# Five loads of the second tile of x as two transfers each, of 120 and of 8 partitions

## The chip, the cores and the metric

The kernel runs on one core of one Trainium2 chip. The metric is the device time of one execution in microseconds (us). The same core has five engines (PE for matrix work, DVE for elementwise work, ACT for copies here, POOL, and SP, which here issues DMAs and nothing else) and 16 DMA engines, which move data between the chip's large memory (HBM) and the on-chip buffer with its 128 partitions.

## The reference

```
# x: (512, 40, 128) float32, W: (128, 128) float32
proj = jnp.einsum('bnd,ed->bne', x, W)
out = proj[:, PAIR_I, :] * proj[:, PAIR_J, :]     # PAIR_I, PAIR_J = np.triu_indices(40, k=1)
```

Each of the 40 features of a batch row is projected by W, and then every one of the 780 pairs of features is multiplied element by element. The output is 512 x 780 x 128 float32, 204.47 MB, against 10.5 MB of input.

## The kernel before

The batch is worked off in four tiles of 128 rows; row b of a tile lives in partition b. A tile of x is 40 features x 128 values per partition. It comes in as ten loads of four features each (`LOADS`, `LOAD_FEATURES`), the last features first: a load moves 2048 bytes (4 x 128 float32) to each of 128 partitions, 256 KB in all. Two buffers, `x_in[0]` and `x_in[1]`, hold an even and an odd tile. Each of the 20 loads (two tiles of ten) has its own semaphore, `x_loaded[half][load]`; a finished transfer adds 16 to it.

- SP issues all 20 loads of the first two tiles first, in one go and without a wait (line 137). After that its loop over the tiles runs: for each of 20 chunks of 39 pairs it waits until DVE has made the chunk (`chunk_ready`) and issues its store (line 145), 19968 bytes from each of 128 partitions, 2496 KB. There are 80 stores. SP's loads and stores stand in one queue.
- ACT issues the loads of the third and fourth tile (line 211), each once the part of the buffer that it overwrites has been read. They stand in ACT's own queue.
- PE turns each feature (line 172, `turn`, which waits for the feature's load at the first of the two groups of a load) and projects it (line 182). ACT copies the results out of the accumulation banks (lines 206 and 217) into `proj`.
- DVE multiplies (line 248). A chunk is written into one of five slots of `products`, and before a slot is written again DVE waits until the store that last read it has landed completely (`stored[slot]`).

SP's last instructions wait until all 80 stores have landed, and that ends the kernel.

Every transfer is cut into packets that the 16 DMA engines work off. A transfer of 128 partitions has 128 data packets, one for each partition, and 16 small packets behind them, one for each DMA engine, that mark the end of that engine's share in the semaphore (called end marks below; a packet of data is 2048 bytes for a load and 19968 bytes for a store).

Of the kernel before, what the change touches and what calls it, by code (L numbers as in the profile page):

```python
# [5 lines left out]
P = 128  # L25
# [6 lines left out]
LOADS = FEATURES // LOAD_FEATURES  # L32
# [2 lines left out]
GROUPS = FEATURES // GROUP  # L35
GROUPS_PER_LOAD = LOAD_FEATURES // GROUP

CHUNK = 39
CHUNKS = PAIRS // CHUNK
SLOTS = 5  # L40
ROUNDS = CHUNKS // SLOTS

assert LOADS * LOAD_FEATURES == FEATURES and GROUPS * GROUP == FEATURES
assert CHUNKS * CHUNK == PAIRS and ROUNDS * SLOTS == CHUNKS and GROUPS % 2 == 0
assert GROUP <= BANK_FEATURES and LOAD_FEATURES % GROUP == 0


def load_range(load):

    return FEATURES - (load + 1) * LOAD_FEATURES, FEATURES - load * LOAD_FEATURES  # L50


def group_range(group):

    return FEATURES - (group + 1) * GROUP, FEATURES - group * GROUP


def chunk_range(chunk):

    return PAIRS - (chunk + 1) * CHUNK, PAIRS - chunk * CHUNK  # L60


def chunk_rows(chunk):

    low, high = chunk_range(chunk)
    rows = []
    for i in reversed(range(FEATURES - 1)):
        a, b = max(low, FIRST_PAIR[i]), min(high, FIRST_PAIR[i + 1])
        if a < b:
            rows.append((i, i + 1 + a - FIRST_PAIR[i], b - a, a - low))  # L70
    return rows


def group_of(i):

    return (FEATURES - 1 - i) // GROUP


def groups_for(chunk):

    return group_of(chunk_rows(chunk)[-1][0]) + 1 if chunk >= 0 else 0


def pairwise_products(nc, x, w, out):
    fp32 = mybir.dt.float32
# [4 lines left out]
    with ExitStack() as ctx:  # L90
        def sbuf(name, shape):
            return ctx.enter_context(nc.sbuf_tensor(name, shape, fp32))
# [4 lines left out]
        def sem(name):  # L97
            return ctx.enter_context(nc.semaphore(name))


        x_in = [sbuf(f"x_in{h}", [P, FEATURES, DIM]) for h in range(2)]
        proj = sbuf("proj", [P, 2, FEATURES, DIM])
        products = [sbuf(f"products{s}", [P, CHUNK, DIM]) for s in range(SLOTS)]
        x_turned = [sbuf(f"x_turned{k}", [DIM, GROUP, P]) for k in range(2)]
        w_in = sbuf("w_in", [DIM, DIM])
        w_turned = sbuf("w_turned", [DIM, DIM])
        identity = sbuf("identity", [P, P])


        turned_ps = [psum(f"turned_ps{k}", [DIM, BANK_FEATURES, P]) for k in range(2)]  # L110
        proj_ps = [psum(f"proj_ps{k}", [P, BANK_FEATURES, DIM]) for k in range(2)]
# [4 lines left out]
        x_loaded = [[sem(f"x_loaded{half}_{k}") for k in range(LOADS)] for half in range(2)]  # L116
# [14 lines left out]
        @block.sync  # L131
        def _(sp):

            for half in range(2):
                for load in range(LOADS):
                    a, b = load_range(load)
                    sp.dma_start(x_in[half][:, a:b, :],
                                 x[half * P:(half + 1) * P, a:b, :]).then_inc(x_loaded[half][load], 16)

            with sp.Fori(0, tiles) as tile:  # L140
                for chunk in range(CHUNKS):
                    a, b = chunk_range(chunk)
                    sp.wait_ge(chunk_ready, tile * CHUNKS + (chunk + 1))
                    sp.nop(nofuse=True)  # L144
                    sp.dma_start(out[bass.ds(tile * P, P), a:b, :],  # L145
                                 products[chunk % SLOTS][:, :, :]).then_inc(stored[chunk % SLOTS], 16)

            for slot in range(SLOTS):
                sp.wait_ge(stored[slot], 16 * tiles * ROUNDS)
# [8 lines left out]
        @block.tensor  # L158
        def _(pe):
            pe.wait_ge(identity_made, 1)  # L160
            pe.wait_ge(w_loaded, 16)
            pe.transpose(w_ps[:, :], w_in[:, :], identity[:, :]).then_inc(w_in_ps, 1)  # L162
            pe.wait_ge(w_ready, 1)

            def turn(pair, half, group):

                if group % GROUPS_PER_LOAD == 0:

                    pe.wait_ge(x_loaded[half][group // GROUPS_PER_LOAD], 16 * pair + 16)
                a, b = group_range(group)  # L170
                for n in range(a, b):
                    last = pe.transpose(turned_ps[group % 2][:, n - a, :], x_in[half][:, n, :], identity[:, :])  # L172
                last.then_inc(group_turned, 1)

            def project(pair, half, group):
                before = pair * 2 * GROUPS + half * GROUPS
                pe.wait_ge(x_turned_ready, before + (group + 1))
                if group >= 2:

                    pe.wait_ge(proj_ready, before + (group - 1))  # L180
                for k in range(GROUP):
                    last = pe.matmul(proj_ps[group % 2][:, k, :], x_turned[group % 2][:, k, :], w_turned[:, :],  # L182
                                     start=True, stop=True)
                last.then_inc(group_projected, 1)


            with pe.Fori(0, tiles // 2) as pair:
                for half in range(2):
                    turn(pair, half, 0)
                    for group in range(1, GROUPS):  # L190
                        turn(pair, half, group)
                        project(pair, half, group - 1)
                    project(pair, half, GROUPS - 1)

                    pe.wait_ge(proj_ready, pair * 2 * GROUPS + (half + 1) * GROUPS)
# [41 lines left out]
        @block.vector  # L237
        def _(dve):
            def multiply_chunk(tile, chunk):
                slot = chunk % SLOTS  # L240
                first_group = groups_for(chunk - 1)
                for i, j, count, place in chunk_rows(chunk):
                    group = group_of(i)
                    if group >= first_group:

                        first_group = group + 1
                        dve.wait_ge(proj_ready, tile * GROUPS + (group + 1))  # L247
                    last = dve.tensor_tensor(  # L248
                        products[slot][:, place:place + count, :],
                        proj[:, tile % 2, i:i + 1, :].broadcast_to([P, count, DIM]),  # L250
                        proj[:, tile % 2, j:j + count, :], ALU.mult)
                last.then_inc(chunk_ready, 1)

            def give_back(tile):

                dve.wait_ge(chunk_ready, tile * CHUNKS + CHUNKS)
                dve.sem_inc(proj_free, 1)  # L257


            dve.sem_inc(proj_free, 2)  # L260

            for chunk in range(CHUNKS):
                if chunk >= SLOTS:

                    dve.wait_ge(stored[chunk % SLOTS], 16 * (chunk // SLOTS))
                multiply_chunk(0, chunk)
            give_back(0)
            with dve.Fori(1, tiles) as tile:
                for chunk in range(CHUNKS):

                    dve.wait_ge(stored[chunk % SLOTS], 16 * ROUNDS * tile + 16 * (chunk // SLOTS))  # L271
                    multiply_chunk(tile, chunk)
                give_back(tile)


# [1 line left out]
_INS = ["r_x", "L0_rec_W"]  # L277
# [17 lines left out]
```

## Time and profile before

| | us |
|---|---|
| time, median of 3 runs | 511.1 |
| time, lowest and highest | 510.85 and 511.14 |
| span of the profiled execution (first to last recorded work of the core) | 508.2 |
| DVE busy | 437.3 |
| PE busy | 71.3 |
| ACT busy | 54.3 |
| one store, from issue to landing, median | 24.0 |

What is recorded of the profiled execution is its span; 511.1 less 508.2 leaves 2.9 us that lie outside it in the timed runs. The page of the profile gives, beside busy times, the mean busy share of the 16 DMA engines and the GB/s that they moved in slices of the span. A share over 1 in a short stretch comes from counting a packet in the stretch in which it starts. The same view can be asked for any stretch, down to that of one packet: one engine of sixteen that is busy gives a share of 0.06.

### The profile page before, as it was taken

To read this page: it belongs to the slowest core of one execution; us is meant where nothing else is said; L and a number is where in the kernel's file an instruction comes from. 1 tells how busy PE (TensorE), PEld (TensorE's weight loads), DVE (VectorE), ACT (ScalarE), POOL (GpSimd) and SP (SyncE) were. 2 spreads that over 40 slices of the span, in tenths; PEclk is the share of its full clock that TensorE was granted. 3 is DMA by queue.
4 is the path that set the end of the run, shared out by engine and by line. 5 is a ranking of instruction groups with operands and counts; after the bars stand their busy time and mean duration, and the time that the engine had idled before them with its cause. 6 is when DMAs were issued, how large, how long until landed. Compare 5 with 4: busy or idle time off the path is not lost.

```text
span 508.2 us, 2204 instructions
## 1 busy us (share of the span) xinstructions
PE 71.3 (14%) x481; PEld 65.4 (13%) x481; DVE 437.3 (86%) x220; ACT 54.3 (11%) x162; POOL 0.7 (0%) x6
## 2 busy tenths in 40 slices
PE   6965100000930000000660000000000000000000
PEld 5854100000920000000660000000000000000000
DVE  3999988888999999899999999999899989999900
ACT  5752000000720000000450000000000000000000
POOL 0000000000000000000000000000000000000000
PEclk9995555555875555555695555555555555555555
DMA  8999999999999999999999999999999999999996
GB/s 311 411 423 433 427 431 428 430 431 434 428 431 432 434 431 432 431 429 434 434 430 432 431 434 432 431 432 432 429 434 431 427 427 427 429 429 431 431 431 277
DMA packets 17430, 215.10 MB, mean 423 GB/s; under 512 B 1936, under 2 KB 2064, under 8 KB 7184
## 3 DMA queue, kind: packets, MB, share of 16 engines
q1 hardware_dynamic: 14400, 209.72, 96.7%
q10 hardware_dynamic: 3024, 5.31, 2.8%
q8 instruction: 2, 0.03, 0.0%
q14 instruction: 4, 0.03, 0.0%
HBM read 10.55 MB, written 204.47 MB: 423 GB/s over the span
## 4 chain that ended last, share of the span: by engine, by line
DMA 68%; DVE 21%; issue 5%; PE 1%; DVEq 0%; SPq 0%; ACT 0%; ACTq 0%
DMA out_dram<-products 67%; DVE products L248 21%; DMA w_in<-in_L_rec_W_dram 1%; PE proj_ps L182 0%; PE turned_ps L172 0%; SPq L145 0%; DVEq L248 0%; PE w_ps L162 0%; ACT proj L217 0%; ACT x_turned L206 0%; DVEq L271 0%; ACT w_turned L201 0%; SPq L144 0%; DVEq L247 0%; ACTq L205 0%
## 5 line engine op out<-in xcount | busy, mean ns | idle before, releaser
L248 DVE TENSOR_TENSOR products<-proj 128x384 f32 (+36 forms) x220 | 437.3, 2045 | 46.3 <-DMA out_dram<-products 37.3
L182 PE MATMUL proj_ps<-w_turned,x_turned 128*128 128x128 f32 x320 | 60.5, 319 | 181.5 <-ACT x_turned L206 181.3
L182 PEld LDWEIGHTS proj_ps<-w_turned,x_turned 128*128 128x128 f32 x320 | 48.9, 219 | 186.3 <-ACT x_turned L206 184.4
L206 ACT COPY x_turned<-turned_ps 128x256 f32<-128x256 f32 x80 | 30.0, 379 | 174.0 <-DVEq L257 171.9
L172 PE MATMUL turned_ps<-identity,x_in 128*128 128x128 f32 x160 | 34.4, 306 | 5.7 <-ACT proj L217 5.1
L217 ACT COPY proj<-proj_ps 128x256 f32<-128x256 f32 x80 | 29.7, 373 | 31.4 <-issue 19.0
L172 PEld LDWEIGHTS turned_ps<-identity,x_in 128*128 128x128 f32 x160 | 23.1, 161 | 6.6 <-issue 5.3
L201 ACT ACT_TABLE_LOAD x1 | 1.3, 1283 | 1.2 <-PEq L284 1.2
L162 PE MATMUL w_ps<-identity,w_in 128*128 128x128 f32 x1 | 0.4, 447 | 4.1 <-DMA w_in<-in_L_rec_W_dram 4.1
L162 PEld LDWEIGHTS w_ps<-identity,w_in 128*128 128x128 f32 x1 | 0.2, 182 | 4.0 <-issue 4.0
L201 ACT COPY w_turned<-w_ps 128x128 f32<-128x128 f32 x1 | 0.3, 265 | 2.1 <-PE w_ps L162 2.1
L155 POOL TENSOR_SCALAR_AFFINE_SELECT identity<-identity 128x128 f32<-128x128 f32 x1 | 0.3, 292 | 0.2 <-POOL identity L153 0.2
L153 POOL MEMSET identity<- 128x128 f32 x1 | 0.2, 204 | 0.3 <-POOLq L284 0.3
L284 POOL MEMSET const-bfloat16-1.0<- 128x1 bf16 x1 | 0.1, 101 | 0.0
L284 POOL MEMSET const-uint8-127<- 128x1 uint8 x1 | 0.1, 101 | 0.0
L284 POOL MEMSET const-float32-0.0<- 128x1 f32 x1 | 0.1, 98 | 0.2 <-issue 0.2
L284 POOL MEMSET const-float32-1.0<- 128x1 f32 x1 | 0.1, 98 | 0.0
## 6 DMA issues: line engine op xcount, KB each, us to landing
out_dram<-products SPq DMA_DIRECT2D x80, 2496.0 KB, 24.0
x_in<-in_r_x_dram SPq DMA_DIRECT2D x20, 256.0 KB, 6.1
x_in<-in_r_x_dram ACTq DMA_DIRECT2D x20, 256.0 KB, 29.8
w_in<-in_L_rec_W_dram ACTq DMA_DIRECT2D x1, 64.0 KB, 3.2
```

The lines of the kernel that those rows point to most:

```text
L153: pool.memset(identity[:, :], 0.0).then_inc(identity_zeroed, 1)
L155: pool.affine_select(out=identity[:, :], in_=identity[:, :], compare_op=ALU.not_equal, fill=1.0, base=0, pattern=[[-1, P]], channel_multip ...
L162: pe.transpose(w_ps[:, :], w_in[:, :], identity[:, :]).then_inc(w_in_ps, 1)
L172: last = pe.transpose(turned_ps[group % 2][:, n - a, :], x_in[half][:, n, :], identity[:, :])
L182: last = pe.matmul(proj_ps[group % 2][:, k, :], x_turned[group % 2][:, k, :], w_turned[:, :], start=True, stop=True)
L201: act.copy(w_turned[:, :], w_ps[:, :]).then_inc(w_ready, 1)
L206: act.copy(x_turned[group % 2][:, :, :], turned_ps[group % 2][:, 0:GROUP, :]).then_inc(x_turned_ready, 1)
L217: act.copy(proj[:, half, a:b, :], proj_ps[group % 2][:, 0:GROUP, :]).then_inc(proj_ready, 1)
L248: last = dve.tensor_tensor(products[slot][:, place:place + count, :], proj[:, tile % 2, i:i + 1, :].broadcast_to([P, count, DIM]), proj[:, ...
L284: nc = _bacc.Bacc("TRN2", target_bir_lowering=False, num_devices=1)
```

## The change

Of the loads of the first two tiles that SP issues, those numbered 5 to 9 of the second tile (`half == 1`, `SPLIT_LOADS`) go as two transfers: the first moves partitions 0 to 119, the second partitions 120 to 127. Both add 16 to the same semaphore, so PE waits for 16 more there, in the first pass over the second tile and in the second pass (the fourth tile), whose loads are issued by ACT and are whole as before. Nothing else is changed; the same bytes go to the same places.

```diff
+WIDE = 120
+SPLIT_LOADS = range(5, LOADS)
...
             for half in range(2):
                 for load in range(LOADS):
                     a, b = load_range(load)
-                    sp.dma_start(x_in[half][:, a:b, :],
-                                 x[half * P:(half + 1) * P, a:b, :]).then_inc(x_loaded[half][load], 16)
+                    if half == 1 and load in SPLIT_LOADS:
+                        sp.dma_start(x_in[1][0:WIDE, a:b, :],
+                                     x[P:P + WIDE, a:b, :]).then_inc(x_loaded[1][load], 16)
+                        sp.dma_start(x_in[1][WIDE:P, a:b, :],
+                                     x[P + WIDE:2 * P, a:b, :]).then_inc(x_loaded[1][load], 16)
+                    else:
+                        sp.dma_start(x_in[half][:, a:b, :],
+                                     x[half * P:(half + 1) * P, a:b, :]).then_inc(x_loaded[half][load], 16)
...
                 if group % GROUPS_PER_LOAD == 0:
 
-                    pe.wait_ge(x_loaded[half][group // GROUPS_PER_LOAD], 16 * pair + 16)
+                    load = group // GROUPS_PER_LOAD
+                    transfers = 2 if half == 1 and load in SPLIT_LOADS else 1
+                    pe.wait_ge(x_loaded[half][load], 16 * pair + 16 * transfers)
```

The instructions that SP issues, in order, from its start to the first store, before. `ISA` and `REGISTER_ALU` are small instructions of the sequencer, among them the wait for a chunk; the shape is that of the side in the on-chip buffer, in elements of 4 bytes.

```order
L131 UNCONDITIONAL_BRANCH
L137 DMA x_in<-in_r_x_dram 128x512 x20
L140 UNCONDITIONAL_BRANCH
L140 ISA
L145 ISA
L145 DMA out_dram<-products 128x4992
```

The same place now:

```order
L120 DMA x_in<-in_r_x_dram 128x512 x15
L115 DMA x_in<-in_r_x_dram 120x512
L117 DMA x_in<-in_r_x_dram 8x512
...
L123 UNCONDITIONAL_BRANCH
L123 ISA
L128 ISA
L128 DMA out_dram<-products 128x4992
```

The rows for 120 and 8 partitions stand there five times in turn: 25 issues ahead of the first store instead of 20. No instruction of another engine moves.

## Rows read from the trace of the kernel before

**Rows 1.** The page: the span in 40 slices, DMA share in tenths, GB/s.
```profile
DMA  8999999999999999999999999999999999999996
GB/s 311 411 423 433 427 431 428 430 431 434 428 431 432 434 431 432 431 429 434 434 430 432 431 434 432 431 432 432 429 434 431 427 427 427 429 429 431 431 431 277
DMA packets 17430, 215.10 MB, mean 423 GB/s; under 512 B 1936, under 2 KB 2064, under 8 KB 7184
...
q1 hardware_dynamic: 14400, 209.72, 96.7%
```
**Rows 2.** The waits: engine and line, releaser: us, times, longest.
```profile
DVE products L248 <- DMA out_dram<-products: 37.3, 64, 1.4
```
**Rows 3.** Busy us of engines by stretch, clock share, DMA share, GB/s.
```profile
6.00:10.00 4.00, 3.90 (x23) 3.72 (x23) 1.11 (x4) 2.46 (x8) 0.00 (x0) 1.00 1.05 400
10.00:20.00 10.00, 10.00 (x85) 9.54 (x84) 10.00 (x11) 8.93 (x29) 0.00 (x0) 1.00 1.06 391
30.00:130.00 100.00, 16.37 (x84) 14.46 (x83) 90.60 (x43) 8.74 (x29) 0.00 (x0) 0.53 1.01 430
430.00:500.00 70.00, 0.00 (x0) 0.00 (x0) 49.06 (x19) 0.00 (x0) 0.00 (x0) 0.50 1.01 429
```
**Rows 4.** Timeline of DVE's end: start us, us, instruction, idle before.
```profile
472.26 5.43 DVE L248 TENSOR_TENSOR products<-proj 128x128 f32 x2 [0.50 <-DMA out_dram<-products]
478.29 5.36 DVE L248 TENSOR_TENSOR products<-proj 128x4992 f32 x1 [0.60 <-DMA out_dram<-products]
```
**Rows 5.** Line 145, the stores: ns min/median/max, first and last start.
```profile
L145 SPq DMA_DIRECT2D out_dram<-products x80: 327/332/359, 15.1 to 483.9; - x80
...
DMA to landing us min/median/max: 13.9/24.0/27.1
```
**Rows 6.** The last packets: stretches of 0.74 us, one store packet long.
```profile
502.70:503.44 0.74, 0.00 (x0) 0.00 (x0) 0.00 (x0) 0.00 (x0) 0.00 (x0) 0.50 0.82 351
...
504.33:505.07 0.74, 0.00 (x0) 0.00 (x0) 0.00 (x0) 0.00 (x0) 0.00 (x0) 0.50 0.19 81
505.07:505.81 0.74, 0.00 (x0) 0.00 (x0) 0.00 (x0) 0.00 (x0) 0.00 (x0) 0.50 0.06 27
505.81:506.55 0.74, 0.00 (x0) 0.00 (x0) 0.00 (x0) 0.00 (x0) 0.00 (x0) 0.50 0.06 27
506.55:507.29 0.74, 0.00 (x0) 0.00 (x0) 0.00 (x0) 0.00 (x0) 0.00 (x0) 0.50 0.06 27
507.29:508.24 0.95, 0.00 (x0) 0.00 (x0) 0.00 (x0) 0.00 (x0) 0.00 (x0) 0.50 0.00 0
```
**Rows 7.** DMA packets that start from 505.56 us to the end.
```profile
DMA packets 3, 0.04 MB, mean 15 GB/s; under 512 B 1, under 2 KB 1, under 8 KB 1
```
**Rows 8.** DMA packets that start between 507.28 and 507.30 us.
```profile
DMA packets 1, 0.00 MB, mean 0 GB/s; under 512 B 1, under 2 KB 1, under 8 KB 1
```
**Rows 9.** Timeline of SP's queue from the start to 24 us.
```profile
0.75 9.87 SPq L137 DMA_DIRECT2D x_in<-in_r_x_dram  x20
15.13 5.79 SPq L145 DMA_DIRECT2D out_dram<-products  x2
```
**Rows 10.** Line 137, the loads: ns, starts, and time to landing.
```profile
L137 SPq DMA_DIRECT2D x_in<-in_r_x_dram x20: 383/432/738, 0.7 to 10.2; - x20
...
DMA to landing us min/median/max: 3.0/6.1/12.1
```
**Rows 11.** Timeline of PE around the second tile.
```profile
22.25 0.66 PE L172 MATMUL turned_ps<-identity,x_in 128*128 128x128 f32 x4 [0.46 <-ACT proj L217]
...
29.55 0.38 PE L172 MATMUL turned_ps<-identity,x_in 128*128 128x128 f32 x2
```

## The prediction

> **What bounds the kernel now.** I read the page's slices first. The DMA share is 9 tenths or more in every slice but the first and the last, at some 430 GB/s, and 215.10 MB go through [rows 1]. No compute engine comes near that. DVE, the busiest, works 90.60 of 100 us in the stretch from 30 to 130 us, while the DMA share is 1.01 [rows 3]. The waits say the same from the other side: DVE waits 64 times for a store to land, 37.3 us in all [rows 2]. One chunk costs DVE 5.36 us [rows 4], one store costs the 16 DMA engines 2496 KB at 430 GB/s [rows 3], 5.9 us with 1 KB as 1024 bytes. A store takes a median of 24.0 us from issue to landing [rows 5], four times its own service, so every DMA engine has about four stores queued. None of them runs dry. The kernel is as long as the work of its DMA engines.
>
> The mean share hides one thing: a transfer has landed when the last engine has done its share, so the end belongs to the slowest single engine, not to the sum. The page counts 1936 packets under 512 bytes [rows 1]. They are the end marks of 80 stores, 40 loads of x and the load of W, 121 transfers, thus 16 marks each: each transfer runs on all 16 engines, with 128/16 = 8 packets per engine. All engines have the same bytes. Do they end together? The stretches of 0.74 us at the end answer [rows 6]. Up to 503.44 us the share is 0.82, 13 engines. Then it falls, and from 505.07 to 507.29 us it is 0.06 in three stretches in a row, 27 GB/s, one store packet each: one engine. Of the packets that start after 505.56 us there are three, two of data and one end mark [rows 7], and that mark starts between 507.28 and 507.30 us [rows 8]. So **15 engines had written their last mark by 505.56 us and one was 1.73 us later**. I call it the laggard. The last landing follows 0.95 us behind its mark (508.24 less 507.29) and is the end of the span.
>
> **The change, part by part.** It touches only how the bytes of five loads are spread over the engines.
>
> *What one engine is spared.* 120 partitions do not go 16 ways evenly, but 15 ways with 8 packets each. I take it that they do, and that one engine has none of them. It is spared five loads of 8 packets. The price of one packet of 2048 bytes comes from the stretch in which loads alone are moved, 10 to 20 us, 391 GB/s over 16 engines, thus 24.4 GB/s for one engine [rows 3]: 84 ns. 5 x 8 x 84 ns = 3.36 us. By the mixed rate of 430 GB/s [rows 3] it would be 76 ns, or 3.05 us. Either is more than 1.73 us.
>
> *What the others get.* 8 partitions are 8 packets. On 8 engines they are one packet more for each in each of five loads: 5 x 84 ns = 0.42 us, and five more end marks, which I cost at nothing since each moves a few bytes (bounds: 0 and, if a mark cost as much as a packet of 2048 bytes, another 0.42 us). All on one engine would be 5 x 8 x 84 ns = 3.36 us there; if that is the engine that was spared, nothing has changed. I take eight engines, as the traffic of every transfer here is spread as widely as its partitions allow.
>
> *Does the spared time reach the end?* Yes, if the engine always has more work queued: it starts on the stores earlier by what it was spared and keeps that lead to its last packet. Its queue holds about four stores [rows 5], 24 us of work, against a lead of 3.4 us over its old self, so it does not run dry. DVE gains nothing and needs nothing: its slot comes free earlier by the same amount.
>
> *What is late next.* If the laggard is the one that is spared, it would write its last mark at about 507.29 - 3.36 = 503.9 us, in the crowd. The end then belongs to the second latest, whose mark is written at or just before 505.56 us: its last data packet falls into the stretch at 504.33 or the one at 505.07 [rows 6]. So the gain is capped at 1.73 us if that engine is not among the eight that get the extra packet, and 1.73 - 0.42 = 1.31 us if it is. Without a row that tells which, I take the middle, 1.5 us, and keep both ends.
>
> *SP.* It issues 25 loads instead of 20. 20 took 9.87 us, 0.49 us each [rows 9]; five more cost 2.5 us, so the loads end at 0.75 + 9.87 + 2.47 = 13.1 us. The first store was issued at 15.13 us, when DVE had its first chunk [rows 9]. 2.0 us of cover remain. If that cover were gone, it would still cost nothing: the last of SP's loads was issued at 10.2 us and took the longest of them, 12.1 us, to land [rows 10], so the engines are busy with loads until about 22 us and a store issued before that only queues.
>
> *PE.* It waits for both transfers of a split load. The first split load is the sixth of the second tile; PE starts that tile at 22.25 us and is still turning its later groups at 29.55 us [rows 11], 7 us after the last load has landed (22.3 us). The wait is met before it is asked. It adds no instruction to a path that bounds, and PE has hundreds of idle us behind that.
>
> The sum: 511.1 - 1.5 = 509.6 us. It is made against the profiled span, 508.2 - 1.5 = 506.7 us, with the 2.9 us outside it unchanged.
>
> **A rule against it.** Rows 1 show that today all 16 engines take part in every transfer. The Trainium skill's page "DMA: Bandwidth & Descriptors", section "Rules for kernel authors", advises against two transfers to disjoint parts of the partitions, since both spread over the same 16 engines; by it the sum would be 511.1 us. The same page, section "Why a DMA increments its semaphore by 16 and not by 1", gives the number of engines as the largest up to 16 that divides the partitions, and on these queues the lowest-numbered ones; by that 120 use 15 and 8 use 8, and the forecast stands if the laggard is the highest-numbered. No row here numbers the engines.
>
> **The rivals.**
>
> *Another engine is the laggard.* Nothing in the rows names the engine that ends last or the one that is spared. If they are two, the laggard ends as before, or 0.42 us later if it gets an extra packet each time: 511.1 to 511.5 us. This also holds if the second transfer's packets all go to the spared engine. For it: 16 engines, one spared. Against it: the spared one is the one at the end of the spread, and an engine that is alone late by more than two store packets must differ in its place from the others; which place is not shown. The Trainium skill's DMA page, section "Latency and other measured facts", calls engines 7 and 15 usually the slower ones, and ties it to another kind of queue; by that the laggard could be the seventh, which gets the extra packets, 511.5 us, or the fifteenth, 509.6 us.
>
> *The 120 partitions go unevenly, on fewer engines (slower).* If the split picks 8 engines with 15 packets each, these have 7 packets more per load and one more from the second transfer, 8 x 5 x 84 ns = 3.36 us more work. With the laggard among them the end moves to 511.1 + 3.4 = 514.5 us; without it, the second latest at 505.56 + 3.36 = 508.9 against 507.29 us, 512.7 us. It decides from 507.29 - 505.56 = 1.73 us of added work on the second latest. Against it: 15 divides 120 with the 8 packets per engine that each transfer has now.
>
> *The lead is not kept.* The laggard falls behind for a reason that follows it, for instance because it shares a path with another engine, and part of the 3.36 us is lost again. It needs to keep only 1.73 us for the full gain; keeping less gives 510.0 to 511.0 us.
>
> **How the numbers follow.** Runs of this kernel lie within 0.3 us of one another, so about 0.2% (1.0 us) can be told from no change. Forecast, 509.2 to 510.0 us: 0.60. Another laggard or all on the spared engine, 511.0 to 511.6 us: 0.25. Lead partly lost, 510.0 to 511.0: 0.08, of which half is faster by over 0.2%. Uneven split, 512.7 to 514.5: 0.07. These give faster 0.64, same 0.29, slower 0.07. The likeliest case alone spans 509.2 to 510.0; the range for 8 in 10 must take in the second case as well: 509.1 to 511.6.
>
> **What would show it.** The page of the changed kernel counts packets under 512 bytes: with 15 and 8 end marks for the two parts, 5 x (15 + 8) - 5 x 16 = 35 more, 1971. If 8 and 8, it stays at 1936; if 16 and 8, 1976. Queue q1 then has 14435 packets. At the end, the three stretches with one busy engine should be gone or be one, and the share should fall from 0.8 to nothing within about 2 us. If the laggard was not the spared engine, these three stretches stand there as before. SP's 25 loads should end at about 13 us, before the first store. DVE's busy time and the duration of its instructions must not move. The forecast is wrong if the page shows 35 more marks and the same tail.

## The result and the profile after

| | before | after |
|---|---|---|
| time, median | 511.1 us | 513.12 us |
| lowest and highest | 510.85 and 511.14 | 512.7 and 513.24 |
| span of the profiled execution | 508.2 us | 510.5 us |
| DVE busy | 437.3 us | 437.5 us |

The changed kernel is **slower, by 2.0 us**: the ratio is 1.0039, with an interval of 1.0027 to 1.005. It was forecast at 509.6 us, faster by 1.5 us, with a range up to 511.6 us.

First the page, its slices and its packets, as in [rows 1]:

```profile
DMA  8999999999999999999999999999999999999995
GB/s 314 365 421 432 426 433 428 427 433 429 432 432 432 429 435 432 432 430 435 430 431 429 433 433 432 427 433 432 435 427 433 432 426 430 429 427 427 427 433 250
DMA packets 17465, 215.10 MB, mean 421 GB/s; under 512 B 1971, under 2 KB 2099, under 8 KB 7219
...
q1 hardware_dynamic: 14435, 209.72, 96.4%
```

There are 1971 packets under 512 bytes, 35 more than before: the ten parts have 15 and 8 end marks, as expected. The split does what it says. But the second slice has fallen from 411 to 365 GB/s, at the same busy share of 9 tenths. From the third slice on the two lines are alike. Closer, the same stretches in both kernels (us from the start; last two columns: DMA share, GB/s). Before:

```profile
0.00:30.00 30.00, 24.52 (x182) 22.38 (x183) 21.11 (x19) 20.85 (x61) 0.70 (x6) 1.00 0.97 370
14.00:20.00 6.00, 6.00 (x52) 5.75 (x52) 6.00 (x6) 5.38 (x18) 0.00 (x0) 1.00 1.07 392
14.00:26.00 12.00, 11.20 (x91) 10.23 (x90) 12.00 (x10) 9.59 (x30) 0.00 (x0) 1.00 1.06 415
```

After, the loads that are split lie in 14 to 20 us; the stretch ahead of it is whole loads alone:

```profile
0.00:30.00 30.00, 24.63 (x178) 22.30 (x179) 20.82 (x19) 20.69 (x60) 0.70 (x6) 1.00 0.98 349
10.00:14.00 4.00, 4.00 (x36) 3.73 (x35) 3.65 (x6) 3.67 (x12) 0.00 (x0) 1.00 1.05 394
14.00:20.00 6.00, 6.00 (x52) 5.64 (x51) 6.00 (x6) 5.35 (x17) 0.00 (x0) 1.00 1.06 311
...
14.00:26.00 12.00, 11.24 (x91) 10.12 (x90) 12.00 (x9) 9.53 (x30) 0.00 (x0) 1.00 1.06 358
30.00:130.00 100.00, 14.69 (x77) 12.78 (x76) 89.01 (x40) 7.93 (x27) 0.00 (x0) 0.54 1.01 430
```

The engines are as busy (1.06) and move less: 358 in place of 415 GB/s over 12 us, 684 KB fewer. At 430 GB/s that is 684/430 = **1.6 us of work left over**; counted over the first 30 us, (370 - 349) x 30 / 430, it is 1.5 us. Nothing gives it back later: from 30 us on both kernels move 430 GB/s, as in [rows 3]. That the share stands above 1 even between 10 and 14 us, where a packet takes 84 ns, is more than the counting of packets at the edges of a stretch can give; so a share is only compared with another share below.

Not only the split loads are slow. The loads that ACT issues are whole and stand in a queue of their own (q10). Between 14 and 20 us, before (first line) and after (packets, MB, share of the 16 engines' time):

```profile
q10 hardware_dynamic: 606, 1.09, 49.6%
...
q10 hardware_dynamic: 461, 0.83, 47.2%
```

Their mean packet, end marks counted, takes 0.496 x 96 us / 606 = 79 ns before and 0.472 x 96 us / 461 = 98 ns after.

Then the end, in stretches of one store packet, as in [rows 6]:

```profile
504.36:505.10 0.74, 0.00 (x0) 0.00 (x0) 0.00 (x0) 0.00 (x0) 0.00 (x0) 0.50 0.63 270
505.10:505.84 0.74, 0.00 (x0) 0.00 (x0) 0.00 (x0) 0.00 (x0) 0.00 (x0) 0.50 0.38 162
505.84:506.58 0.74, 0.00 (x0) 0.00 (x0) 0.00 (x0) 0.00 (x0) 0.00 (x0) 0.50 0.25 108
506.58:507.32 0.74, 0.00 (x0) 0.00 (x0) 0.00 (x0) 0.00 (x0) 0.00 (x0) 0.50 0.06 27
507.32:508.06 0.74, 0.00 (x0) 0.00 (x0) 0.00 (x0) 0.00 (x0) 0.00 (x0) 0.50 0.06 27
508.06:508.80 0.74, 0.00 (x0) 0.00 (x0) 0.00 (x0) 0.00 (x0) 0.00 (x0) 0.50 0.06 27
508.80:509.54 0.74, 0.00 (x0) 0.00 (x0) 0.00 (x0) 0.00 (x0) 0.00 (x0) 0.50 0.06 27
```

The tail with one busy engine is still there, four stretches where there were three. The laggard was not relieved. SP's queue has emptied sooner than was reckoned: its loads end at 11.9 us, the first store goes out at 15.51 us.

```profile
11.53 0.35 SPq L117 DMA_DIRECT2D x_in<-in_r_x_dram  x1
15.51 5.82 SPq L128 DMA_DIRECT2D out_dram<-products  x2
```

### The profile page after: what moved, and what is told of

Its sections match the earlier page's. It is cut to its first block, busy times and chain, and to the rows that moved or that the text cites. A ratio compares the mean times of both kernels' runs of the same rounds, so it can differ in the third digit from the quotient of the medians.

```text
span 510.5 us, 2211 instructions
## 1 busy us (share of the span) xinstructions
PE 70.8 (14%) x481; PEld 64.4 (13%) x481; DVE 437.5 (86%) x220; ACT 54.2 (11%) x162; POOL 0.7 (0%) x6
## 2 busy tenths in 40 slices
DMA packets 17465, 215.10 MB, mean 421 GB/s; under 512 B 1971, under 2 KB 2099, under 8 KB 7219
## 3 DMA queue, kind: packets, MB, share of 16 engines
q1 hardware_dynamic: 14435, 209.72, 96.4%
## 4 chain that ended last, share of the span: by engine, by line
DMA 67%; DVE 21%; issue 5%; PE 1%; DVEq 0%; SPq 0%; ACT 0%; ACTq 0%
DMA out_dram<-products 67%; DVE products L232 21%; DMA w_in<-in_L_rec_W_dram 1%; PE proj_ps L167 1%; PE turned_ps L157 0%; SPq L128 0%; DVEq L232 0%; PE w_ps L145 0%; ACT proj L201 0%; ACT x_turned L190 0%; DVEq L254 0%; ACT w_turned L185 0%; SPq L127 0%; DVEq L231 0%; ACTq L189 0%
## 5 line engine op out<-in xcount | busy, mean ns | idle before, releaser
L232 DVE TENSOR_TENSOR products<-proj 128x384 f32 (+36 forms) x220 | 437.5, 2045 | 48.4 <-DMA out_dram<-products 39.3
```

Source lines behind the costliest of these rows:

```text
L232: last = dve.tensor_tensor(products[slot][:, place:place + count, :], proj[:, tile % 2, i:i + 1, :].broadcast_to([P, count, DIM]), proj[:, ...
```

## The experiments

Two things had to be told apart: what makes the engines slow between 14 and 22 us, and where the laggard is. Theory A: the partitions over which a transfer reaches, and which engine gets which of them, set how fast they are written. Theory B: a second transfer costs time as such. Unless the text says otherwise the base is the changed kernel; the times of the kernel before, taken beside theirs, are medians of 510.87 to 510.94 us. All GB/s below are of the stretch from 14 to 26 us, 415 before, where no other is named.

**Even parts: 64 and 64.**

```diff
-WIDE = 120
+WIDE = 64
```

> The five loads go as partitions 0 to 63 and 64 to 127 instead of 120 and 8; both parts divide evenly over 16 engines (4 packets each), so no engine is spared and none gets more bytes. Theory A (packets get slow when a transfer's partitions are dealt to the engines in another way than a whole load's: 115 to 120 ns instead of 88 in the trace after): here the dealing is different too, so 12 to 20 us should show packets well over 88 ns, GB/s under 350, and 512.5 to 514 us. Theory B (a second transfer costs time as such, some 0.4 us for each of five): 513 us, packets themselves at 88 ns. Theory C (only the uneven split over 15 engines hurts): 511.1 us.

512.82 against 510.94 us, ratio 1.0037 [1.0023, 1.0051].

```profile
14.00:20.00 6.00, 6.00 (x52) 5.64 (x51) 6.00 (x6) 5.38 (x17) 0.00 (x0) 1.00 1.07 286
...
14.00:26.00 12.00, 11.17 (x90) 10.01 (x89) 12.00 (x9) 9.67 (x30) 0.00 (x0) 1.00 1.07 346
```

No engine is spared here, and none gets more bytes, yet the loss is nearly that of the change. Theory C falls. The arithmetic of the stretch holds again: (415 - 346) x 12 / 430 = 1.9 us, and 1.88 us were measured. A and B are both left.

**Fewer transfers: the 8-partition parts as one.**

```diff
+                        if load == SPLIT_LOADS[0]:
+                            sp.dma_start(x_in[1][WIDE:P, 0:b, :],
+                                         x[P + WIDE:2 * P, 0:b, :]).then_inc(x_loaded[1][load], 16)
                         sp.dma_start(x_in[1][0:WIDE, a:b, :],
                                      x[P:P + WIDE, a:b, :]).then_inc(x_loaded[1][load], 16)
-                        sp.dma_start(x_in[1][WIDE:P, a:b, :],
-                                     x[P + WIDE:2 * P, a:b, :]).then_inc(x_loaded[1][load], 16)
...
```

PE waits for two transfers only at the first of the five loads.

> The 120-partition parts stay as five transfers; the 8-partition parts of all five loads go as one transfer (10240 bytes for each of 8 partitions) ahead of them: 6 transfers in place of 10, same bytes. Theory A (the 120-partition packets are slow): as the changed kernel, 512.8 to 513.3 us, packets of 2048 bytes at 115 ns from 14 us on. Theory B (cost of added transfers, five of them, 2.0 us): one fifth of it is left, 511.3 to 511.7 us.

513.7 against 510.94 us, ratio 1.0051 [1.0034, 1.0067].

```profile
14.00:26.00 12.00, 11.19 (x90) 10.20 (x89) 12.00 (x10) 9.57 (x30) 0.00 (x0) 1.00 1.07 313
```

Four transfers fewer, and 0.6 us slower than the change. Theory B would have it at 511.5 us, so the number of transfers isn't what costs. That it came out above theory A's range too was a hint that eight engines writing 10240 bytes each to eight adjacent partitions at once are slow themselves.

**The small parts alone, beside whole loads** (added work; their data are not used). The base is the kernel before.

```diff
+                    if half == 1 and load >= 5:
+                        sp.dma_start(products[4][0:8, a:b, :], x[0:8, a:b, :]).then_inc(extra, 16)
...
```

DVE waits for these transfers before it first writes that slot.

> All loads whole as before; behind each of loads 5 to 9 of the second tile an extra transfer of 8 partitions x 2048 bytes into a part of a product slot that is not in use yet (added work, its data are not used). Theory A: small transfers cost only their packets, at most 5 x 84 ns = 0.42 us: 511.1 to 511.6 us, packets at 88 ns. Theory B: five added transfers cost what the change cost, 513 us.

511.17 against 510.94 us, ratio 1.0006 [0.9996, 1.0015], and 411 GB/s:

```profile
14.00:26.00 12.00, 11.22 (x91) 10.17 (x89) 12.00 (x9) 9.59 (x31) 0.00 (x0) 1.00 1.06 411
```

The five small transfers cost 0.2 us in the median, within the forecast bounds of 0 and 0.42, and the interval takes in both. So, by elimination, most of the loss in the change is with the parts of 120 partitions; no run has these parts alone, and the small parts here go to partitions 0 to 7 instead of 120 to 127.

**The same two transfers, even and odd partitions.** This is the run that decides between the theories. Everything is as with 64 and 64, but for which partitions go together:

```diff
-                        sp.dma_start(x_in[1][0:WIDE, a:b, :],
-                                     x[P:P + WIDE, a:b, :]).then_inc(x_loaded[1][load], 16)
-                        sp.dma_start(x_in[1][WIDE:P, a:b, :],
-                                     x[P + WIDE:2 * P, a:b, :]).then_inc(x_loaded[1][load], 16)
+                        sp.dma_start(x_in[1][0:P:2, a:b, :],
+                                     x[P:2 * P:2, a:b, :]).then_inc(x_loaded[1][load], 16)
+                        sp.dma_start(x_in[1][1:P:2, a:b, :],
+                                     x[P + 1:2 * P:2, a:b, :]).then_inc(x_loaded[1][load], 16)
```

> As the run with 64 and 64 partitions, but the first transfer takes the even and the second the odd partitions; number of transfers, of packets for each engine, and bytes are the same. Theory A, in the form 'a transfer over a narrow range of partitions cannot be taken in at full rate, since the on-chip buffer takes in data by groups of partitions': the even ones reach over all 128 partitions, so packets go back to about 88 ns, GB/s from 14 to 20 us back to about 390, time 510.9 to 511.4 us. Theory B (any split in two costs, or any other dealing of partitions to engines): as with 64 and 64, 512.7 to 513 us and 280 GB/s.

510.92 against 510.87 us, ratio 1.0004 [0.9994, 1.0013]: the loss is gone (nine of the ten runs took 510.66 to 511.52 us, one 512.75).

```profile
14.00:20.00 6.00, 6.00 (x52) 5.74 (x52) 6.00 (x6) 5.38 (x17) 0.00 (x0) 1.00 1.10 409
...
14.00:26.00 12.00, 11.22 (x90) 10.17 (x90) 12.00 (x9) 9.60 (x30) 0.00 (x0) 1.00 1.05 416
```

286 GB/s became 409 between 14 and 20 us. Theory B is out: a second transfer as such costs nothing here. Nor is it SP's time for the issues, since an issue takes SP 0.60 us in this run as with 64 and 64. One thing moves along with the partitions: each transfer now reads every second row of x from HBM instead of adjacent rows. This run can't tell the place that is read from the place that is written; runs further below do, for transfers of 8 partitions.

**The split on loads that run alone.** Loads 2 to 6 of the first tile instead, while ACT has almost nothing queued.

```diff
-SPLIT_LOADS = range(5, LOADS)
+SPLIT_LOADS = range(2, 7)
...
-                    if half == 1 and load in SPLIT_LOADS:
+                    if half == 0 and load in SPLIT_LOADS:
...
```

The two transfers and PE's wait are those of the first tile accordingly.

> The 120 and 8 split is made on loads 2 to 6 of the first tile, which go through the engines while nothing else does (before ACT's loads start to share at about 9 us), instead of loads 5 to 9 of the second. Theory A: the rate of the split transfers by themselves is seen; between 4.5 and 9 us GB/s well under the 400 of whole loads, about 220 to 300, five loads 1.5 to 3 us later, end 512.5 to 514 us. Theory B2 (the slow packets need ACT's loads in the same stretch, that is, two queues mixed): 390 to 400 GB/s as before, end 511.1 us or less.

512.81 against 510.87 us, ratio 1.0037 [1.0025, 1.0049].

```profile
4.00:6.00 2.00, 1.42 (x5) 0.90 (x5) 0.00 (x0) 0.46 (x2) 0.00 (x0) 1.00 0.99 288
6.00:9.00 3.00, 2.90 (x14) 2.77 (x14) 0.29 (x1) 1.52 (x5) 0.00 (x0) 1.00 1.05 271
```

Whole loads move 402 GB/s from 6 to 9 us:

```profile
6.00:9.00 3.00, 2.90 (x15) 2.76 (x15) 0.29 (x1) 1.52 (x5) 0.00 (x0) 1.00 1.04 402
```

271 GB/s without a second queue of any weight: the slowness is the transfers' own.

**And 64 and 64 there.** The edit is the last one with `WIDE = 64`.

> As the last one, with 64 and 64 partitions. Theory A: if partitions 0 to 63 reach only half of the ways into the buffer, the rate between 4.5 and 9 us is at least half of 400 GB/s (each half alone) and at most 400 (if the two halves overlap in the queues): 200 to 330 GB/s. Theory B2: 390 to 400 GB/s.

513.56 against 510.87 us, ratio 1.0053 [1.0033, 1.0073].

```profile
4.00:6.00 2.00, 1.36 (x5) 0.90 (x5) 0.00 (x0) 0.40 (x2) 0.00 (x0) 1.00 0.77 235
6.00:9.00 3.00, 2.90 (x13) 2.71 (x13) 0.29 (x1) 1.52 (x5) 0.00 (x0) 1.00 0.85 239
```

Some 240 GB/s, 60% of 402, but this run does not show that adjacent halves bring the engines down to that. The busy share is 0.77 and 0.85, where 120 and 8 had 0.99 and 1.05: here the engines were short of work. SP needs longer for the issue of a half than for that of a whole load, 0.60 us against 0.43 [rows 10]:

```profile
L115 SPq DMA_DIRECT2D x_in<-in_r_x_dram x5: 552/596/597, 1.7 to 6.7; - x5
...
DMA to landing us min/median/max: 3.2/3.6/4.1
```

A half is issued every 0.64 us, and 131072 bytes in 0.64 us are 205 GB/s. Each landed 3.2 to 4.1 us after its issue, and the quickest load of before took 3.0 us [rows 10]: little stood queued ahead of it. Even and odd halves, which were not run here, would have met the same limit. That the packets were slow besides can be estimated: 0.85 of busy share at 239 GB/s is 1.37 times as much engine time for each byte as 1.04 at 402, which would leave 402 / 1.37 = 293 GB/s to engines that are kept busy, near the 286 GB/s of the second tile. There the halves stand behind 15 loads issued before them, and the share is 1.07.

**Two extra transfers of 8 partitions, ahead of the second tile's loads.** Meant to find the laggard by giving eight engines 1.48 us more (added work; the data are not used). The base of this run and of all that follow is the kernel before; the diffs of the next four show the line that differs from the run ahead of them.

```diff
+                if half == 1:
+                    for slot in (3, 4):
+                        sp.dma_start(products[slot][0:8, :, :], x[0:8, 0:CHUNK, :]).then_inc(extra, 16)
...
```

DVE waits for both before it first writes these slots.

> All loads whole as before; ahead of the second tile's loads two extra transfers of 8 partitions x 19968 bytes into product slots 3 and 4 before they are in use (added work, data not used): 2 x 0.74 = 1.48 us more for 8 engines if the 8 partitions go to 8 engines. If the engine that ends last (1.73 us behind the second latest) is one of these 8: 512.5 to 512.7 us, and 1.5 us more between it and the others. If it is not: 511.1 to 511.3 us, with the eight 1.5 us closer to the end. All packets stay at 84 to 88 ns in either case if the slow packets of the change come from the transfers of 120 partitions.

516.39 against 510.94 us, ratio 1.0104 [1.0088, 1.0121]: 5.4 us, nearly four times the price of its packets, and outside what was expected.

```profile
10.00:14.00 4.00, 4.00 (x36) 3.81 (x35) 4.00 (x6) 3.54 (x13) 0.00 (x0) 1.00 0.97 104
```

The engines are busy (0.97) and move 104 GB/s. The added 2 x 8 x 19968 bytes are 319 KB; 319 KB in 5.4 us is 59 GB/s, about what two engines do alone (27 GB/s each [rows 6]). Eight engines with one narrow goal hold up the other loads as well, whole as those are.

**The same bytes to spread partitions.**

```diff
-                        sp.dma_start(products[slot][0:8, :, :], x[0:8, 0:CHUNK, :]).then_inc(extra, 16)
+                        sp.dma_start(products[slot][0:127:18, :, :], x[0:8, 0:CHUNK, :]).then_inc(extra, 16)
```

> As the run with two extra transfers of 8 partitions x 19968 bytes, which cost 5.4 us, but the 8 destination partitions are 0, 18, 36 and so on to 126 instead of 0 to 7 (added work, data not used); the 8 rows that are read are the same. Theory A (narrow destination): GB/s from 10 to 16 us stays near 390 instead of falling to 103, and the time is 512.4 to 512.7 us if the engine that ends last is one of the eight, 511.0 to 511.3 us if not. If reading 8 adjacent rows, or eight engines at work at all, were what cost the time: 516 us again.

513.48 against 510.87 us, ratio 1.0052 [1.0035, 1.0068].

```profile
10.00:14.00 4.00, 4.00 (x35) 3.83 (x34) 3.61 (x6) 3.53 (x11) 0.00 (x0) 1.00 1.01 264
```

The rows that are read are the same ones, so it is the place written to that cost 2.8 of the 5.4 us. But 264 GB/s isn't 390: spreading alone does not clear it, and 2.6 us is neither of the two results expected.

**The same bytes, each engine on its own partitions.** The Trainium skill's page "SBUF — State Buffer", section "Door 1: The DMA port swizzle", says that the partitions form 16 groups of eight, such as 0 to 3 with 32 to 35, or 4 to 7 with 36 to 39, each behind a port of its own. The page "DMA: Bandwidth & Descriptors", section "The descriptor swizzle", says that in a transfer of 128 partitions each engine has one such group. By both, engines 0 to 7 own partitions 0, 4, 8 and so on to 28:

```diff
-                        sp.dma_start(products[slot][0:127:18, :, :], x[0:8, 0:CHUNK, :]).then_inc(extra, 16)
+                        sp.dma_start(products[slot][0:32:4, :, :], x[0:8, 0:CHUNK, :]).then_inc(extra, 16)
```

> Loads whole; two extra transfers of 8 partitions x 19968 bytes as in the run with spread partitions, but to partitions 0, 4, 8 and so on to 28 (added work, data not used). Theory A2 (each DMA engine of a whole transfer writes a group of partitions of its own, and the split costs because engines meet on one group): by the Trainium skill's page SBUF - State Buffer, section on the DMA port swizzle, these eight partitions lie in eight groups, and each is that of the engine that gets it; by A2 nobody meets anybody, GB/s from 10 to 14 us stays near 390, 8 engines end 1.48 us later and 8 do not. Then the last engine tells which half it is in: end at 512.3 to 512.6 us if among the eight, 510.9 to 511.2 us if not. If A2 is wrong and any 8-partition transfer is slow: 513.5 us as with partitions 0, 18, 36.

512.12 against 510.88 us, ratio 1.003 [1.0018, 1.0043].

```profile
10.00:14.00 4.00, 4.00 (x36) 3.73 (x35) 4.00 (x6) 3.54 (x12) 0.00 (x0) 1.00 0.98 364
```

Its count of packets (16 more under 512 bytes than before, for two transfers):

```profile
DMA packets 17462, 215.42 MB, mean 423 GB/s; under 512 B 1952, under 2 KB 2080, under 8 KB 7200
```

The page of the profile counts 8 end marks for each of these transfers in all three runs. For the same bytes from the same rows on the same number of engines: 104, 264, 364 GB/s, and 5.4, 2.6, 1.2 us. By the two pages, if the eight engines are 0 to 7 in the order of the partitions, partitions 0 to 7 lie in two groups; 0, 18, 36 and so on lie in eight, but all save the first belong to another engine than the one that writes them; 0, 4, 8 and so on lie in eight, each its own engine's. The three results stand in that order, so the rules agree with all three; no run here numbers the engines. The end moved by 1.24 us of the 1.48 put on eight engines, so the laggard is very likely one of the eight. An engine outside them would hardly have moved: over the first 30 us this run has 368 GB/s against 370 before, 60 KB fewer, and at 430 GB/s that is 0.14 us. With four partitions and with two:

```diff
+                        sp.dma_start(products[slot][0:16:4, :, :], x[0:4, 0:CHUNK, :]).then_inc(extra, 16)
```

> The same with 4 partitions, 0, 4, 8, 12: four engines get 1.48 us more. End at 512.3 to 512.6 us if the engine that ends last is one of the four, 510.9 to 511.2 us if not.

510.94 against 510.88 us, ratio 1.0011 [0.9995, 1.0027] (one of the ten runs took 514.75 us, the others 510.62 to 511.64).

```diff
+                        sp.dma_start(products[slot][0:8:4, :, :], x[0:2, 0:CHUNK, :]).then_inc(extra, 16)
```

> The same with 2 partitions, 0 and 4: two engines get 1.48 us more. End at 512.3 to 512.6 us if the engine that ends last is one of the two, 510.9 to 511.2 us if not.

510.92 against 510.88 us, ratio 1.0002 [0.9992, 1.0011]. Four engines can have 1.48 us more work and the time does not move clear of the noise. The laggard is among those that the 8-partition transfer has and the 4-partition one has not. If the k of a transfer's engines are always the first k, that is the fifth to the eighth; which one was not tried.

**Stores in halves.** 20 of the 80 stores, with the counts that DVE and SP wait for raised to match:

```diff
+                    if chunk // SLOTS == 2:
+                        for h in range(2):
+                            sp.dma_start(out[bass.ds(tile * P + 64 * h, 64), a:b, :],
+                                         products[chunk % SLOTS][64 * h:64 * h + 64, :, :]).then_inc(
+                                             stored[chunk % SLOTS], 16)
+                    else:
...
```

> Not the loads but 20 of the 80 stores (chunks 10 to 14 of each tile) go as two transfers, of partitions 0 to 63 and 64 to 127. If the narrow range binds only what is written into the on-chip buffer (theory W): 430 GB/s stays, 511 us. If it binds what is read from it as well (theory R): while such stores are served the rate falls as it did for the loads, 430 to about 280 or, with nothing wide beside them, 218 GB/s, so 20 stores cost 9.1 to 11.7 us each in place of 5.9 us: 575 to 627 us at most; with the queues of the engines running apart and mixing both halves, less, but more than 515 us.

604.47 against 510.9 us, ratio 1.1823 [1.1737, 1.191]. Stretches of 10 us in the second tile, where SP issues the halves from 214 to 252 us, and one wait of DVE:

```profile
200.00:210.00 10.00, 0.00 (x0) 0.00 (x0) 9.04 (x4) 0.00 (x0) 0.00 (x0) 0.50 1.00 425
...
220.00:230.00 10.00, 0.00 (x0) 0.00 (x0) 5.43 (x2) 0.00 (x0) 0.00 (x0) 0.50 0.97 248
230.00:240.00 10.00, 0.00 (x0) 0.00 (x0) 5.43 (x2) 0.00 (x0) 0.00 (x0) 0.50 0.95 280
...
270.00:280.00 10.00, 0.00 (x0) 0.00 (x0) 4.84 (x2) 0.00 (x0) 0.00 (x0) 0.50 0.62 214
280.00:290.00 10.00, 0.00 (x0) 0.00 (x0) 4.26 (x3) 0.00 (x0) 0.00 (x0) 0.50 0.70 276
290.00:300.00 10.00, 0.00 (x0) 0.00 (x0) 7.11 (x2) 0.06 (x1) 0.00 (x0) 0.50 0.65 276
...
275.15 5.43 DVE L254 TENSOR_TENSOR products<-proj 128x384 f32 x2 [10.00 <-DMA out_dram<-products]
```

93.6 us for 20 stores, 4.7 us on each one's 5.9. Theory W, with 511 us, is out: reading from adjacent halves of the on-chip buffer is no free thing either. Two parts of the 93.6 us can be seen. At first the engines are busy (0.97 and 0.95) at 248 and 280 GB/s. Later, while DVE still waits up to 10.0 us for halves to land, the share is 0.62 to 0.70: about a third of the engines' time goes unused, since DVE, busy 9.04 of 10 us ahead of the halves, gets its slots late and has little ready for the next store. Theory R fits, but its cause is argued here and not shown: stores in even and odd partitions were not run, so neither a split of a store as such nor the place that is written in HBM is ruled out.

## Why the prediction was wrong, point by point

- **What bounds the kernel**: right. Only the DMA engines' work moved the time; DVE's 437.5 us and the 430 GB/s of the stores are as before, and the losses of the runs with loads are found as GB/s missing in one stretch.
- **What the change does**: right. 1971 small packets and 14435 in the queue, as worked out.
- **The price of one packet**: this step failed, and it was the costly one. I took 84 ns for a packet of 2048 bytes from whole loads and gave it to the packets of a transfer with other partitions. Where the split transfers run alone, they move 271 GB/s against 402. Worked out from share and rate, a packet there takes 1.05 x 16 x 2048 / 271 = 127 ns, and 85 ns in whole loads (1.04 and 402). Five loads of 8 packets for each engine at 43 ns more are 1.7 us, where the sum had nothing; in the changed kernel the 684 KB that are missing between 14 and 26 us are 1.6 us. The sum's only added work was that of the eight engines, and the prediction looked for no bound of the 120-partition packets, although rows 1 to 11 have no transfer that is not 128 partitions wide. With no row for it, its rate was an unknown cost and belonged in the range.
- **The laggard is the engine that is spared, and the end moves forward by 1.31 to 1.73 us**: failed as well. The tail shows one busy engine in four stretches, where it should have been none or one. The rival "another engine is the laggard" named this tail, with 511.1 to 511.5 us, and the runs with extra work on eight and on four engines fit it. They put the laggard among the eight engines of an 8-partition transfer; that the engine spared by the 120-partition part is not one of these eight is the rule quoted in the prediction, which no run tests. Were it one of them, the rival "the lead is not kept" would fit the same tail. Either way the 3.36 us of spared packets bought nothing at the end.
- **The eight extra packets, 0.42 us**: the run that adds them alone measured 0.2 us, its interval reaching from none to 0.8 us. If the laggard is one of the eight, 1.6 + 0.42 = 2.0 us makes up the 2.02 us that were measured. That close a fit is partly luck. Only the 1.6 is read from rows; in the run with one 8-partition transfer the same sum gives (415 - 313) x 12 / 430 + 0.42 = 3.3 us, and 2.8 were measured, so the 0.42 may well be less.
- **SP and PE**: right in effect. The ten issues took SP 0.40 us each instead of 0.49, and 3.6 us of cover remained.
- **The time outside the span**: I took 2.9 us. In every later run the time is 2.2 us above the span (513.12 against 510.9 is one of them), so the profiled run of before was itself 0.7 us shorter than its median run. The tail differs from run to run as well. Before, one engine is busy alone in three stretches of 0.74 us [rows 6]; in the run with even and odd partitions, at the same median time, in four:

```profile
505.00:505.74 0.74, 0.00 (x0) 0.00 (x0) 0.00 (x0) 0.00 (x0) 0.00 (x0) 0.50 0.06 27
505.74:506.48 0.74, 0.00 (x0) 0.00 (x0) 0.00 (x0) 0.00 (x0) 0.00 (x0) 0.50 0.06 27
506.48:507.22 0.74, 0.00 (x0) 0.00 (x0) 0.00 (x0) 0.00 (x0) 0.00 (x0) 0.50 0.06 27
507.22:507.96 0.74, 0.00 (x0) 0.00 (x0) 0.00 (x0) 0.00 (x0) 0.00 (x0) 0.50 0.06 27
```

  So three against four says nothing of the change by itself, and a gap of 1.73 us read from one execution was less firm a cap than I made it.
- **The slower rival**: it had the right sign for another reason (fewer engines with more packets). The engines did get 15 and 8 shares; what was slow was each packet.

What stays open: which of the engines is the laggard, and why it is slower. And no version came out faster. No run took work off the laggard and left the other packets at their speed, so what that would be worth is still not known.

## What to carry to other kernels

Keep the large transfers between HBM and the on-chip buffer 128 partitions wide. If a load has to be cut, cut it along the free dimension, as the ten loads of a tile are here, or take every second partition, not adjacent halves; for a store every second partition was not tried. Where the DMA engines bound a kernel, look at GB/s beside their busy share, since here a busy share of 1.06 or 1.07 stood for 415 as for 313 GB/s. A low share in the same line says something else: the engines are short of work, as with 64 and 64 in the first tile, where SP's issues set the rate. And before moving work off the engine that ends last, find out by added work which engine that is, and price a packet in the kind of transfer that it will be part of.

## What the runs showed of the hardware

- With five loads cut into adjacent halves of the partitions the rate between 14 and 20 us falls from 392 to 286 GB/s; cut into even and odd ones it is 409. Cut into 120 and 8, loads that run alone fall from 402 to 271.
- Sixteen packets of 19968 bytes to eight adjacent partitions bring all 16 engines down to 104 GB/s for the four us shown.
- Slow packets of one queue slow the other queue too: the mean packet of ACT's whole loads took 98 ns between 14 and 20 us in place of 79.
- 20 stores in adjacent halves cost 93.6 us, part of it at 248 to 280 GB/s, part of it with the engines only 0.62 to 0.70 busy.
- For loads the cost is that of placement, not of the number of transfers: five more transfers, each on 16 engines, cost 0.05 us in the median.
- SP needs 0.60 us to issue a load of 64 partitions, and 0.43 us for one of 128 (medians), so halves issued into empty queues came at 205 GB/s.
- The rule of the Trainium skill that I weighed against the change (page "DMA: Bandwidth & Descriptors", section "Rules for kernel authors") says of two transfers to disjoint partition halves that they are not worth it, since they share the same engines. The runs agree with the advice. I had read it as a time that stays unchanged, and adjacent halves cost 1.9 us.
